# Layer norm deviations by one pow, token rows in one store, and a new order of the first rounds in a vision tower kernel

## The chip, the core and the metric

The kernel runs on one NeuronCore of a Trainium2 chip, as one program. The metric is device time in microseconds, the median of several executions. TensorE is called PE here, VectorE DVE, ScalarE ACT, GpSimd POOL and SyncE SP.

## What is computed

```python
h = tok(x, ...)                          # 16 images x 256 tokens x 512 features, an SSM kernel as token mixer
h = concat([cls_tok, h], axis=1)         # 16 x 257 x 512
h = h + attn(layernorm(h), ...)          # gates = ln(u) @ W_in + b; scan over tokens; @ W_out; plus u @ W_skip
h = h + ffn(layernorm(h), ...)           # 8 experts, 2 per token, and a shared expert

def layernorm(x, eps=1e-5):
    return (x - mean(x)) / sqrt(var(x) + eps)
```

The attention step normalises once more: its own layer norm acts on the already normalised row. With v the variance of a row, the first norm divides by sqrt(v + eps), and the second by sqrt(v/(v + eps) + eps).

## The kernel before, in words

Three parts run one after the other. **Setup** (lines 283 to 523) converts all weights of the attention step and of the shared expert into pairs of f16 halves (SP loads, ACT makes the high half, DVE the low half, line 480), builds tables for the token mixer, and ends in a barrier of all engines. SP's last work in it is to write the 7 blocks of empty rows of `x_slots` (lines 303 to 310): seven stores of zeros, a wait, seven stores of 128 single words each, a wait.

**Rounds** (from line 706): every engine runs `body(k)` for k = -1 to 17. Rounds 2 to 13 are a loop, the others are unrolled. `iterate` (line 629) does this. Chunk n of 256 rows (chunk 0: 128 rows with the class token) passes through several rounds:

- in round n-2 the token mixer makes it: DVE computes tables `tok_e` (line 1225) and products `tok_p` (line 1247, six steps f = 0 to 5), PE multiplies (`features`, line 942), ACT copies the result to `hst` (`tok_out`, line 1116), SP stores it to `h_tok` in HBM (line 795);
- in round n-1 SP loads it back as `hx` (line 760), DVE takes its statistics (`stats2`, line 1397), POOL works out the deviations (lines 850 to 859, ten instructions that wait for each other, three of them pow), DVE normalises (line 1445), ACT and DVE split it into f16 halves (`x2r`, lines 1161 and 1450), PE transposes and multiplies with `W_in`, and DVE scans (`scan`, line 1325);
- in round n PE multiplies with `W_skip` and `W_out` (`project`), DVE adds the residual `hc` with the factor `ir` (lines 1467 and 1468), takes statistics for each tile of 128 rows, POOL works out the deviation (lines 882 to 884), DVE normalises (`normed`), ACT and DVE split (`rows_hi`, `rows_lo`), PE transposes, and the router follows;
- in round n+1 PE and ACT run the shared expert, DVE chooses the experts (`choose`, `place`), and POOL scatters the rows to `x_slots` with indirect DMAs (line 872).

Each engine's order is written out by hand in `body`, and semaphores join them. ACT's order in a round is: silu(0) (activation of the shared expert's columns), the high half of yT, silu(1), the copy of `ir`, the residual copy `hx` to `hc` (line 1149, semaphore `c_prom`), the rest of the shared expert, `x2r`, and so on. SP may only overwrite `hx` with the next chunk when `c_prom` says that the copy is done, when the store of that chunk has landed (`c_hst`), and when `c_lo2` says that the old chunk is split. Behind this load on SP's queue stand the store of converted expert weights and the loads of the next ones.

**Experts** (from line 1085): 71 tiles of 128 rows, with transposing loads, matmuls, and an indirect DMA that adds to the result. The change does not touch them, nor the final copies to `out`.

## Time and profile before

| what | value |
| --- | --- |
| median of 3 runs | 1319.91 us (1319.89 to 1320.18) |
| the profiled execution | 1316.03 us |
| its span, which the rows count from | 1314.3 us |
| setup | 0 to 61.9 us |
| round -1, to the start of scan(0) | 61.9 to 91.4 us |
| round 0, from there to scan(1) | 91.4 to 131.0 us |
| round 1 | 131.0 to 174.2 us |
| rounds 2 to 13, the loop | about 44.1 us each |
| experts' first matmul | 859.8 us |

Times in rows are microseconds from the start of the span unless a column says ns. A line number is that of the kernel before. Where one row joins several instructions, x says how many. What stands in square brackets at the end of a row is how long the engine stood idle before it, and which instruction released it.

### The profile page before, as it was taken

The numbers are of one execution on the slowest core, as the hardware profiler recorded it, in microseconds if no ns is written. First come the engines' busy times: TensorE is split into PE (matmuls) and PEld (weight loads), VectorE is DVE, ScalarE is ACT, GpSimd is POOL, SyncE is SP. The second block draws the span as 40 slices with busy tenths as digits, with TensorE's granted clock in tenths as the row PEclk, the third lists the DMA queues.
The fourth block names the chain that finished last, engine by engine and source line by source line (L and its number), as shares of the span: only waits on it lengthen the run. The fifth ranks groups of instructions, "written<-read, shape, count | busy, mean of one in ns | idle before, by whom it ended". The sixth has DMA issues, their size and how long they took to land.

```text
span 1314.3 us, 28311 instructions
## 1 busy us (share of the span) xinstructions
PE 1096.3 (83%) x8330; PEld 720.8 (55%) x8331; DVE 847.0 (64%) x2171; ACT 356.6 (27%) x675; POOL 459.0 (35%) x519
## 2 busy tenths in 40 slices
PE   2045799998999899989999998769999999999970
PEld 2034467566655765676567755535555555555540
DVE  7855788888888888888888765524344444444440
ACT  4312243324332433244324432201111111111110
POOL 1012321432143224322432231115555555555550
PEclk8556899999999999999999999889999999999995
DMA  5510233333333323332333239659997788878868
GB/s 181 153 32 17 75 107 110 97 116 115 101 110 117 115 86 122 120 115 76 129 123 116 81 127 406 238 134 177 218 195 132 127 129 131 132 128 133 131 95 264
DMA packets 238515, 174.51 MB, mean 133 GB/s; under 512 B 186162, under 2 KB 204978, under 8 KB 236164
## 3 DMA queue, kind: packets, MB, share of 16 engines
q1 hardware_dynamic: 221924, 128.54, 37.7%
q0 software_dynamic: 15504, 36.46, 13.9%
q10 hardware_dynamic: 1040, 8.91, 1.7%
q8 instruction: 25, 0.41, 0.1%
q14 instruction: 22, 0.18, 0.1%
HBM read 61.59 MB, written 88.12 MB: 114 GB/s over the span
## 4 chain that ended last, share of the span: by engine, by line
PE 40%; DVE 26%; issue 10%; DMA 6%; ACT 4%; POOL 3%; SPq 2%; POOLq 1%; DVEq 1%; ACTq 0%
PE bank L1077 9%; PE bank L1067 9%; PE bank L1068 8%; PE bank L930 6%; PE bank L1011 4%; DMA mixed<-h_tok 3%; DVE wexp L1257 3%; DVE wexp L1273 2%; DVE h L1467 2%; DVE h L1468 2%; DVE stat L1470 2%; POOL sc L882 1%; DVE wexp L1237 1%; DMA sums<-x2w,rows_in 1%; PE bank L952 1%
## 5 line engine op out<-in xcount | busy, mean ns | idle before, releaser
L930 PE MATMUL bank<-wexp 128*128 128x256 f16 (+2 forms) x3252 | 419.7, 288 | 26.0 <-DVE gf L1280 13.7
L930 PEld LDWEIGHTS bank<-wexp 128*128 128x128 f16 x3252 | 309.0, 100 | 114.3 <-issue 20.5
L1067 PE MATMUL bank<-wexp,rows_in 128*128 x852 | 256.0, 313 | 10.8 <-issue 4.5
L1068 PE MATMUL bank<-wexp,rows_in 128*128 x852 | 255.4, 313 | 0.0
L908 POOL DMA_INDIRECT sums<-x2w,rows_in x71 | 113.8, 1602 | 119.8 <-DMA sums<-x2w,rows_in 76.0
L896 POOL TENSOR_TENSOR ex<-base,ld 128x8 f32<-128x8 f32 x71 | 120.5, 1697 | 80.4 <-DVE ld L1512 80.0
L1533 DVE SCALAR_TENSOR_TENSOR mixed<-bank,mixed 128x352 f32<-128x352 f32 x71 | 37.3, 525 | 163.0 <-ACT mixed L1214 126.5
L1011 PE MATMUL bank<-wexp 128*128 128x512 f16 x495 | 112.5, 380 | 17.0 <-DVE wexp L1273 15.5
L1067 PEld LDWEIGHTS bank<-wexp,rows_in 128*128 128x128 f16 x852 | 83.2, 98 | 69.2 <-issue 29.4
L850 POOL TENSOR_SCALAR sc<-mv 128x2 f32<-128x2 f32 x17 | 5.5, 321 | 317.6 <-DVE mv L1409 317.6
L1214 ACT ACTIVATE mixed<-bank 128x352 f32<-128x352 f32 x71 | 32.9, 463 | 304.7 <-PE bank L1068 285.3
L1077 PE MATMUL bank<-wexp,gates 128*128 (+1 forms) x477 | 111.7, 379 | 3.2 <-DMA gates<-mixed 1.7
L1068 PEld LDWEIGHTS bank<-wexp,rows_in 128*128 128x128 f16 x852 | 83.3, 98 | 44.0 <-issue 0.3
L872 POOL DMA_INDIRECT x_slots<-x3w,sl x66 | 81.1, 1229 | 70.9 <-DVE sl L1323 40.3
L1011 PEld LDWEIGHTS bank<-wexp 128*128 128x128 f16 x495 | 45.8, 98 | 73.6 <-issue 16.8
L1125 ACT ACTIVATE sgs<-bank 128x256 f32<-128x256 f32 (+1 forms) x102 | 38.1, 373 | 157.5 <-PE bank L930 157.5
L1257 DVE TENSOR_TENSOR wexp<-wexp 128x1024 f32 (+1 forms) x64 | 77.9, 1220 | 2.3 <-issue 1.9
L1077 PEld LDWEIGHTS bank<-wexp,gates 128*128 128x128 f16 (+1 forms) x477 | 46.6, 98 | 53.3 <-issue 4.5
L938 PE MATMUL bank<-ident,x2w 128*128 128x128 f16 x264 | 18.9, 228 | 65.6 <-DVE x2w L1450 54.8
L952 PE MATMUL bank<-wexp 64*128 64x64 f32 x1024 | 68.8, 290 | 4.4 <-DVE wexp L1262 4.4
L882 POOL TENSOR_SCALAR sc<-mv 128x1 f32<-128x1 f32 x33 | 22.9, 694 | 134.6 <-DVE mv L1472 134.6
L952 PEld LDWEIGHTS bank<-wexp 64*128 64x128 f32 x1024 | 66.5, 206 | 4.9 <-DVE wexp L1262 4.9
(250 smaller groups left out, 1469.2 us busy)
## 6 DMA issues: line engine op xcount, KB each, us to landing
w_halves<-rows_in SPq DMA_DIRECT2D x16, 704.0 KB
wexp<-w_halves ACTq DMA_DIRECT2D x1, 8704.0 KB
wexp<-w_halves SPq DMA_DIRECT2D x8, 1088.0 KB
h_tok<-tokens SPq DMA_DIRECT2D x128, 64.0 KB, 2.5
mixed<-h_tok SPq DMA_DIRECT2D x16, 512.0 KB, 4.2
sums<-r_o SPq DMA_DIRECT2D x16, 512.0 KB, 2.8
out<-sums SPq DMA_DIRECT2D x16, 512.0 KB, 11.0
x_slots<-zrow SPq DMA_DIRECT2D x8, 792.0 KB, 11.9
```

Source lines behind the costliest of these rows:

```text
L872: nc.gpsimd.indirect_dma_start(out=xs_d.bitcast(I32), out_offset=bass.IndirectOffsetOnAxis(ap=sl[:, i, c:c + 1], axis=0), in_=x3w[:, i, :] ...
L896: nc.gpsimd.tensor_tensor(ex[:, b % 2, 0, :], base[:], ld[:, b % 2, :], ALU.pow).then_inc(d_ex, 1)
L908: nc.gpsimd.indirect_dma_start(out=rs_d, out_offset=bass.IndirectOffsetOnAxis(ap=ext[b][:, E:E + 1].bitcast(I32), axis=0), in_=yo[b % 2][: ...
L930: last = MM(dst, stat_of(step, a), mov_of(step, b), start=(s_ == 0 and a + b == 0), stop=(s_ == len(steps) - 1 and a == 1))
L952: last = MM(BU[t][:, j * NA:(j + 1) * NA], pp[q, f, j].rearrange("p b c -> p (b c)"), ea[q, f, j, :], start=(f == 0), stop=(f == 1))
L1011: MM(BD[:], gT[:, m, a, t], wsd[:, m, b, :], start=(m == 0 and a + b == 0), stop=False)
L1067: MM(GB[:, 0:H], xT[b][:, a, c, :], wexp[:, u, o:o + H], start=s_, stop=e_)
L1068: last = MM(UB[:, 0:H], xT[b][:, a, c, :], wexp[:, u, o + H:o + 2 * H], start=s_, stop=e_)
L1077: last = MM(DB[:], gT2[b % 4][0:HK[c], a, c, :], wexp[0:HK[c], bass.ds(unit, 2), o:o + D // 2], start=(c == 0 and a + w == 0), stop=(c == ...
L1125: A(sgs[P - p1:P, m % 2, 0:w], BU[m % 2][0:p1, 0:w], ACT.Silu, scale=SXW).then_inc(c_sg, 1)
L1257: ch.do(TT((pp, pt)[f % 2][:, f // 2], cc, hh, ALU.mult))
L1533: STT(gx[:], UB[:, 0:H], SXW, sg[:], ALU.mult, ALU.mult).then_inc(d_gf, 1)
```

## The change

What it does, in eight edits:

- **One pow.** DVE computes `var2`, two columns for each of two tiles: v(1 + eps) + eps squared, and v + eps, with two `tensor_scalar` instructions behind the statistics. POOL takes one pow with exponent -0.5 over all four. The result's first half is the combined deviation of both norms. In place of ten POOL instructions there is one. The factor `SX` moves into the split: ACT's copy scales, and DVE's subtraction becomes `scalar_tensor_tensor`. The same for the second norm of a chunk: `var3` on DVE, one pow on POOL, for each tile.
- **ir on DVE.** The residual's factor is made by two DVE instructions ahead of `scan`, in place of pow, multiply (POOL) and copy (ACT).
- **One store of tokens.** `h_tok` is laid out so that each of the 128 partitions of `hst` writes one run of 4 KB: one DMA in place of eight. The load back then reads runs of 256 B in place of 2 KB, in two DMAs.
- **Residual copy first.** ACT copies `hx` to `hc` at the head of its round.
- **First features first.** In round -1 DVE does all six `tok_p` steps of chunk 1 directly behind the statistics of chunk 0 and ahead of its normalisation, PE does `features` at the head of the round, and ACT does `tok_out` at the head of the round. `tok_e(1)` moves from ahead of the round to ahead of the statistics.
- **Empty rows early.** Two stores (one of 1.8 MB, one of 64 B runs) ahead of the weight loads in place of fourteen behind them.
- DVE's and POOL's waits on buffers that no longer exist go.
- The counts of chained instructions per loop round follow (POOL 14 to 1, DVE 47 to 49).

The core of the diff:

```diff
+                sp.wait_ge(p_gp, 17)
+                none = xs_d[ZERO:ZERO + ZT * P, :].bitcast(I32).rearrange("(z p) w -> p z w", p=P)
+                sp.dma_start(none[:, :, 0:D], zrow[:].bitcast(I32)[:, 0:D]...broadcast_to([P, ZT, D])).then_inc(p_z, 16)
+                sp.dma_start(none[:, :, D:D + 16], zt[:]).then_inc(p_z, 16)
                 for i, (kind, src, n) in enumerate(jobs):
...
-                for z in range(ZT):
-                    sp.dma_start(none[:, z, :], zrow[:].bitcast(I32)).then_inc(p_z, 16)
-                sp.wait_ge(p_z, 16 * ZT)
-                for z in range(ZT):
-                    sp.dma_start(none[:, z, D + E:D + E + 1], zt[:, z:z + 1], allow_slow_non_contiguous=True).then_inc(p_z, 16)
-                sp.wait_ge(p_z, 32 * ZT)
+                sp.wait_ge(p_z, 32)
# SP: load and store of tokens
-                        sp.wait_ge(c_hst, n * NB * 16)
+                        sp.wait_ge(c_hst, n * 16)
-                        sp.dma_start(hx[:], src).then_inc(c_hx, 16)
+                        src = hs_d[bass.ds(n - 1, 1)].rearrange("q b i p a -> p (q i) b a")
+                        for i in range(2):
+                            sp.dma_start(hx[:, i, :].rearrange("p (b a) -> p b a", a=NA), src[:, i]).then_inc(c_hx, 16)
...
-                        for b in range(NB):
-                            sp.dma_start(dst[b], hst[b * B:(b + 1) * B].rearrange("c j t a -> c (j t) a")).then_inc(c_hst, 16)
+                        dst = hs_d[bass.ds(n - 1, 1)].rearrange("q b i (c t) a -> (q b i c) (t a)", t=TC)
+                        sp.dma_start(dst, hst[:].rearrange("p j t a -> p (j t a)")).then_inc(c_hst, 16)
# POOL
-                        link(TS(sc[:, 0, :], mv[:, 0, :, 1], EPS, None, ALU.add))
-                        link(TT(sc[:, 1, :], sc[:, 0, :], pwc[:, 0, :], ALU.pow))
...
-                        TS(sc[:, 3, :], sc[:, 3, :], SX, None, ALU.mult).then_inc(c_pw2, 1)
+                        TT(inv2[:], var2[:], power[:], ALU.pow).then_inc(c_pw2, 1)
...
-                            link(TS(sc[:, 5, i:i + 1], mv[:, 1, i, 1:2], EPS, None, ALU.add))
-                            link(TT(sc[:, 6, i:i + 1], sc[:, 5, i:i + 1], pwc[:, 0, 0:1], ALU.pow))
-                            TS(sc[:, 6, i:i + 1], sc[:, 6, i:i + 1], SX, None, ALU.mult).then_inc(c_pw3, 2 // nt)
+                            TT(inv3[:, i:i + 1], var3[:, i:i + 1], power[:, 0, 0:1], ALU.pow).then_inc(c_pw3, 2 // nt)
# PE
+                    if isinstance(k, int) and k == -1:
+                        features(k)
...
-                    if htok(k + 2):
+                    if htok(k + 2) and not (isinstance(k, int) and k == -1):
                         features(k)
# ACT
-                    A(x3r[:, i, 0, :], xf[:, i, :], ACT.Copy).then_inc(c_hi3, 2 // nt)
+                    A(x3r[:, i, 0, :], xf[:, i, :], ACT.Copy, scale=SX).then_inc(c_hi3, 2 // nt)
...
                 def body(k):
+                    if isinstance(k, int) and k == -1:
+                        tok_out(1, 0)
+                        tok_out(1, 1)
+                    if has(k):
+                        n, nt = k, tiles(k)
+                        act.wait_ge(c_hx, (n + 1) * 32)
+                        at_least(act, c_oev, n * 2)
+                        A(hc[:, 0:nt, :], hx[:, 0:nt, :], ACT.Copy).then_inc(c_prom, 1)
                     if has(k - 1):
                         silu(k - 1, 0)
...
-                        act.wait_ge(c_hx, (n + 1) * 16)
-                        act.wait_ge(c_pw2, n + 1)
-                        at_least(act, c_oev, n * 2)
-                        A(ir[:], sc[:, 4, :], ACT.Copy).then_inc(c_irc, 1)
-                        A(hc[:, 0:nt, :], hx[:, 0:nt, :], ACT.Copy).then_inc(c_prom, 1)
# DVE
-                        last.then_inc(c_st2, 1)
+                        last.then_inc(c_vr2, 1)
+                        v.wait_ge(c_vr2, n + 1)
+                        TS(var2[:, 0, :], mv[:, 0, :, 1], 1.0 + EPS, EPS * EPS, ALU.mult, ALU.add)
+                        TS(var2[:, 1, :], mv[:, 0, :, 1], EPS, None, ALU.add).then_inc(c_st2, 1)
...
+                        if m == 0 and isinstance(k, int) and k == -1:
+                            for f in range(5):
+                                tok_e(1, f)
                         if m == 0 and has(k + 1):
                             stats2(k + 1)
+                        if m == 0 and isinstance(k, int) and k == -1:
+                            for f in range(6):
+                                tok_p(1, f)
...
-                        TT(x2r[:, 0:nt, 1, :], xf[:, 0:nt, :], x2r[:, 0:nt, 0, :], ALU.subtract).then_inc(c_lo2, 1)
+                        STT(x2r[:, 0:nt, 1, :], xf[:, 0:nt, :], SX, x2r[:, 0:nt, 0, :], ALU.mult, ALU.subtract).then_inc(c_lo2, 1)
...
-                            nc.vector.bn_aggr(mv[:, 1, i, :], stat[:, 1, i, :]).then_inc(c_st3, 2 // nt)
+                            nc.vector.bn_aggr(mv[:, 1, i, :], stat[:, 1, i, :]).then_inc(c_vr3, 2 // nt)
+                            v.wait_ge(c_vr3, n * 2 + (i + 1) * 2 // nt)
+                            TS(var3[:, i:i + 1], mv[:, 1, i, 1:2], EPS, None, ALU.add).then_inc(c_st3, 2 // nt)
...
                     if has(k + 1):
+                        link(STT(irt[:], inv2[:, 0, :], SXW, inv2[:, 1, :], ALU.mult, ALU.mult))
+                        link(TT(ir[:], irt[:], var2[:, 0, :], ALU.mult))
                         scan(k + 1)
```

## Rows read from the trace of the kernel before

**Rows 1.** The page: granted PE clock by slice, and the chain's shares by engine.

```profile
PEclk8556899999999999999999999889999999999995
...
PE 40%; DVE 26%; issue 10%; DMA 6%; ACT 4%; POOL 3%; SPq 2%; POOLq 1%; DVEq 1%; ACTq 0%
```

**Rows 2.** Busy time in one loop round: length, PE, PEld, DVE, ACT, POOL, clock, DMA.

```profile
483.90:528.00 44.10, 40.44 (x358) 28.44 (x357) 36.78 (x84) 15.75 (x30) 13.68 (x21) 1.00 0.34 110
```

**Rows 3.** Setup, SP: the stores of single words (timeline), and one load (DMA issues).

```profile
57.23 3.18 SPq L309 DMA_DIRECT2D x_slots<-zt  x7
...
st<-in_L_attn_W_in SPq DMA_DIRECT2D x1, 768.0 KB, 10.2
```

**Rows 4.** Timeline at the end of setup: ACT's last work, DVE's last work, DVE's next.

```profile
54.82 3.92 ACT L367 ACTIVATE wexp<-pe 128x1024 f32<-128x1024 f32 x2
...
57.04 0.69 DVE L480 SCALAR_TENSOR_TENSOR wexp<-xj,wexp 64x512 f16<-64x512 f32 x1
61.95 0.07 DVE L1496 MEMSET carry<- 128x16 f32 x1 [4.22 <-PEq L189]
```

**Rows 5.** Timeline of round -1: normalisation of chunk 0, features of chunk 1, scan(0).

```profile
75.64 0.55 DVE L1445 TENSOR_SCALAR wexp<-mixed,mv,sc 128x512 f32<-128x512 f32 x1 [4.78 <-POOL sc L859]
...
80.37 7.09 PE L952 MATMUL bank<-wexp 64*128 64x64 f32 x64 [1.17 <-DVE wexp L1262]
...
91.41 0.23 DVE L1330 TENSOR_SCALAR gates<-gates 128x128 f32<-128x128 f32 x1 [2.52 <-ACT gates L1200]
```

**Rows 6.** Timeline of round 0: store and load of chunk 1, its statistics, normalisation, scan(1).

```profile
88.60 5.29 SPq L795 DMA_DIRECT2D h_tok<-tokens  x8
95.84 0.40 SPq L760 DMA_DIRECT2D mixed<-h_tok  x1
...
99.48 1.29 DVE L1402 BATCH_NORM_STATS2 stat<-mixed 128x6 f32<-128x512 f32 x2 [3.77 <-DMA mixed<-h_tok]
...
108.30 1.00 DVE L1445 TENSOR_SCALAR wexp<-mixed,mv,sc 128x512 f32<-128x512 f32 x2 [4.89 <-POOL sc L859]
...
131.03 0.29 DVE L1330 TENSOR_SCALAR gates<-gates 128x256 f32<-128x256 f32 x1 [5.62 <-ACT gates L1200]
```

**Rows 7.** Windows with a load alone, then a store alone; last columns DMA share, GB/s.

```profile
96.50:99.40 2.90, 2.90 (x9) 0.98 (x8) 0.00 (x0) 0.00 (x0) 0.00 (x0) 0.50 0.55 181
...
125.20:130.30 5.10, 5.10 (x48) 4.22 (x47) 0.21 (x1) 1.00 (x2) 0.00 (x0) 0.79 0.44 75
```

**Rows 8.** Groups by line and form: busy us, mean ns, idle before them.

```profile
L896 POOL TENSOR_TENSOR ex<-base,ld 128x8 f32<-128x8 f32 x71 | 120.5, 1697 | 80.4 <-DVE ld L1512 80.0
...
L1315 DVE TENSOR_TENSOR rt<-oh,rt 128x16 f32<-128x16 f32 x32 | 5.6, 175 | 1.1
```

**Rows 9.** Timeline of one loop round, by engine.

```profile
498.47 1.22 DVE L1257 TENSOR_TENSOR wexp<-wexp 128x1024 f32 x1
...
510.98 1.19 DVE L1262 TENSOR_TENSOR wexp<-wexp 128x1024 f32<-128x1024 f32 x1
513.55 0.55 DVE L1352 TENSOR_SCALAR wexp<-h,mv,sc 128x512 f32<-128x512 f32 x1 [1.38 <-issue]
...
520.91 0.55 DVE L1352 TENSOR_SCALAR wexp<-h,mv,sc 128x512 f32<-128x512 f32 x1 [1.30 <-POOL sc L884]
...
521.49 0.63 ACT L1114 ACTIVATE x3w<-wexp 128x512 f16<-128x512 f32 x1 [0.78 <-DVE wexp L1352]
...
497.97 0.71 POOL L855 TENSOR_TENSOR sc<-sc,pwc 128x2 f32<-128x2 f32 x1 [0.18 <-POOL sc L854]
...
502.05 0.22 POOL L859 TENSOR_SCALAR sc<-sc 128x2 f32<-128x2 f32 x1 [0.20 <-POOL sc L858]
...
511.29 0.98 POOL L882 TENSOR_SCALAR sc<-mv 128x1 f32<-128x1 f32 x1 [1.77 <-DVE mv L1472]
...
502.72 3.41 PE L1011 MATMUL bank<-wexp 128*128 128x512 f16 x15 [1.05 <-DVE wexp L1273]
```

**Rows 10.** Timeline of round 15: the statistics of the last chunk.

```profile
756.93 1.29 DVE L1402 BATCH_NORM_STATS2 stat<-mixed 128x6 f32<-128x512 f32 x2 [1.50 <-DMA mixed<-h_tok]
```

More of the change, by code:

```diff
@@ L45 @@
 UNROLL = 8
-PER_POOL, PER_DVE = 14, 47
+PER_POOL, PER_DVE = 1, 49
 def at_least(eng, sem, value):
@@ L550, in vit_tower @@
         mv = sb("mv", [P, 2, 2, 2], F32)
-        sc = sb("sc", [P, 8, 2], F32)
-        pwc = sb("pwc", [P, 2, 2], F32)
+        var2 = sb("var2", [P, 2, 2], F32)
+        inv2 = sb("inv2", [P, 2, 2], F32)
+        var3 = sb("var3", [P, 2], F32)
+        inv3 = sb("inv3", [P, 2], F32)
+        irt = sb("irt", [P, 2], F32)
+        power = sb("power", [P, 2, 2], F32)
         ir = sb("ir", [P, 2], F32)
@@ L1267, in tok_p, with tokens_p @@
                             ch.do(ins)
+                def tokens_p(k, f):
+                    if not isinstance(k, int) or k >= 0:
+                        tok_p(k + 2, f)
                 def glow(n, m):
```

59 lines of the change are left out of this document (22 added, 37 removed).

## The prediction

> **What bounds the kernel now.** I read the page first. Its chain of work is 40% PE and 26% DVE, with 10% "issue", 6% DMA and 3% POOL [rows 1]: no engine bounds the whole, so the change has to be priced stage by stage. The granted PE clock is at 0.5 in the second and third slices (33 to 98 us) and mostly full from the fifth [rows 1], so in the first rounds PE runs at its 1.2 GHz level. Then the timelines of each engine, stage by stage. *Setup*: ACT ends at 58.74 and DVE at 57.73, but the barrier opens only at 61.95, after SP's single-word stores that are issued until 60.41 [rows 3, 4]. *Rounds -1 and 0* are one serial chain: statistics, POOL's ten instructions, normalisation, features, store, load, statistics, POOL again [rows 5, 6]. *Loop rounds*: 44.1 us each, of which PE is busy 40.44 and DVE 36.78, and DVE's many short dependent steps leave it few real gaps [rows 2]. DVE and PE hand the path to each other: PE waits 1.05 us for a DVE result at 502.72, DVE waits 1.38 and 1.30 us for the second norm's deviation [rows 9]. *Experts*: untouched; they shift as a block.
>
> **Setup.** The empty rows leave the end. The barrier then waits for ACT (58.74) plus the 0.4 us that lie between the last store and DVE's start: DVE starts at 59.15, **-2.8 us**. The other side: 1.8 MB now stands ahead of the weight loads. At the 350 GB/s that loads reach this is about 5 us, with the 64 B runs about 6, so W_in lands at 22 and not 15.7 [rows 3]. What hides it: the beta matmuls and the last x transposes slip to about 26, ACT's second conversion to 28, and DVE asks for these halves only from 32.5 on; the loads of the second half of setup wait on DVE anyway. Cover left is some 6 us; past that it costs one for one. Floor: DVE's own end 57.73 gives -3.8; if cover fails, 0. SP waits for one more POOL memset and an iota (0.3 us), behind ten DMA issues: nothing.
>
> **Round -1.** DVE: statistics of chunk 0 come 1.15 us earlier in the order (one tok_p moves behind), so from 63.5; mean and variance are there at 64.65, two small instructions add 0.35, and six tok_p of 1.19 (the row at 510.98 is one) [rows 9] take 7.1: features can start at 72.15 instead of 80.37 and end 7.1 us later [rows 5], at 79.25. POOL's pow is finished under them. What is late next: ACT has tok_out ahead of x2r's high half, so that half waits until 80.35 although its input is ready at 72.7. Then 0.63 for it, 0.7 for the low half, 1.25 to the copy of the transposes, 1.0 for this copy, 3.3 for the W_in matmuls and 0.7 for tanh: scan(0) at 88.0 instead of 91.41 [rows 5], **-3.4 in all**.
>
> **Round 0.** The store (one issue) lands by about 85 and no longer matters. The load of chunk 1 now waits for the residual copy, which ACT reaches behind tanh: 88.0 to 88.6. Price of the load: before, 3.6 us from issue to statistics [rows 6], with 1.6 us of work per DMA engine (share 0.55 of 2.9 us, 256 runs of 2 KB, so 100 ns each) [rows 7]. A 256 B run costs 23 ns by the window with a store alone (share 0.44 x 16 x 5.1 us over 1530 runs) [rows 7], so 2048 runs take 3.0 us per engine: 2.0 fixed, 3.0, and 0.3 for the second issue give 5.3. Ends: 4.2, and 7.8 if a load of this grain goes at the pace of the eight stores (5.29 us plus landing) [rows 6]. I take 5.3, since the engine share is nearer to what limits one big DMA. Statistics at 93.95 (99.48 before). From there to the normalisation it was 8.82 us [rows 6], with ten POOL instructions. Now: 1.7 to the variance, 0.3 for var2, 2.33 for two tok_p, under which the pow of four columns (between 0.71 for two and 1.70 for eight [rows 8, 9], so 1.04) is hidden: 4.25. Normalisation at 98.2 instead of 108.30, -10.1; var3 in front of the last tok_p gives 0.1 back. scan(1) starts at 121.0 instead of 131.03 [rows 6]: **-10.0 in all**.
>
> **Round 1.** PE leads, partly at the lower clock. var2 (0.28) lies on the DVE stretch that feeds PE, and the two ir instructions (0.40) stand between the last split and scan(2): **+0.7**. The pow gains vanish behind PE and ACT.
>
> **A loop round.** DVE gains work: two var2 instructions after the wait (0.28), var3 twice (0.20 each), irt and ir (2 x 0.20), priced by dependent small ones of 0.175 plus 0.03 of hand-over [rows 8]. scalar_tensor_tensor costs what tensor_tensor did. What leaves: for the first tile the way from variance (511.06) to normalisation (513.55) [rows 9] was three POOL instructions. Now var3 ends at 511.26, tok_p runs to 512.37, and the pow ends up to 0.58 behind it. *Why not earlier*: the instruction at 511.29 takes 0.98 us where it needs 0.23, and it ends 0.10 after DVE's tok_p [rows 9]. POOL stands still while DVE reads two SBUF operands; a pow of 0.71 at most, held back like this, ends 0.71 - 0.23 + 0.10 behind. So 512.95, a gain of 0.6, and the same for the second tile (520.91). The Trainium skill, "SBUF — State Buffer", section "SBUF: two separate sides", says just this of a DVE instruction with two SBUF inputs, and more: the one that starts first holds the pair for the whole instruction, so a pow could stop DVE too.
>
> Now the path. irt and ir delay scan, hence gprod(0) and PE, by 0.40; var2 by another 0.28. PE waits for DVE's last glow (1.05) [rows 9] and then has no gap until features end, so features end about 0.7 later, and with them ACT's copies. Up to the first normalisation DVE is 0.68 late and gets 0.6 back: about even. The second one could be 0.6 early, but ACT, which splits it at 521.49, is busy with tok_out and the transposes until 521.35: only **-0.13** is left [rows 9]. Twelve loop rounds and round 14: -1.7. Bounds: -0.6 per round if PE's delay is absorbed, +0.4 if the small instructions cost half as much again and the tile gains are lost.
>
> **Hidden in the loop**: POOL's ten instructions, ready at 502.27 just before DVE wants them at 502.6 [rows 9]; the residual copy at ACT's head, which lies in 3.1 us of idle before silu(0); the load of hx, which can now go at 483 and is needed at 493.9, so 11 us of cover for 5.3; the expert weights' transfers behind it on SP, which only move forward by 5 us; the scatters, that start earlier.
>
> **End.** In round 15 the statistics wait 1.50 us for the load [rows 10]. The earlier copy takes that away; PE becomes the limit and lets 1.0 through. In round 16 nothing of DVE covers the second tile's deviation: 0.56. Together **-1.6**.
>
> **Sum** against the profiled execution: -10.0 + 0.7 - 1.7 - 1.6 = -12.6, so 1316.0 becomes 1303.4. The median of the runs lies 3.9 above the profiled one; the same step from it gives 1307.3.
>
> **Rivals.**
> 1. *PE absorbs the small DVE steps*, so that both tile gains count: -0.6 in 14 rounds instead of -0.13, 1301. For it: DVE's two stalls of 1.3 us are plain. Against: PE is busy 40.44 of 44.1 [rows 2]. Chance 0.16.
> 2. *The rounds give back most of it*: +0.4 per round (7 us), or the start gains 5 less because the load takes 7.8 and the clock rises later: 1312 to 1317. Chance 0.16.
> 3. *DVE is stopped by the pow.* A four-column pow (1.04) that starts first would hold back the DVE subtraction beside it in each of 14 rounds: +15, 1322, no change. In the trace POOL's pow at 497.97 ran until 498.68 while a two-operand DVE instruction started at 498.47 and took its usual 1.2 us [rows 9], which speaks against it. The Trainium skill's page on SBUF named above would have it so. Chance 0.05.
> 4. *The price of a run is fixed* (slower than before). If a run of 256 B costs the 100 ns of a 2 KB run [rows 7], a load takes 2048/16 x 0.1 + 2 = 14.8 us. Up to 11 us it is hidden in the loop; above, each round pays: 3.8 x 14 = 53, and the start 9.5: 1370. Against it stand the 23 ns. The Trainium skill, "DMA: Bandwidth & Descriptors", asks in "Specifications" for 512 B or more, without a price for this case. Chance 0.05.
> 5. *The edit does not do what it says*: features first but the chain to scan(0) unchanged. It is counted in 2.
>
> **How the numbers follow.** Forecast 0.58 (1303 to 1312), rivals 0.16, 0.16, 0.05, 0.05. The range 1297 to 1318 leaves out rivals 3 and 4 and a tail of the first. A measurement of this kernel tells about 0.2% (2.6 us) from no change: faster 0.87, same 0.07, slower 0.06.
>
> **What would show it.** In the new profile: DVE's first memset at 59.2; features from 72; scan(0) at 88, scan(1) at 121; the load of chunk 1 issued at about 88.6 and landed 5.3 later; loop rounds of 44.0; the second-norm wait of DVE 0.7 us instead of 1.38; pow of four columns about 1.04 when free. Wrong if the rounds are longer than 44.5 or shorter than 43.6, if the load takes over 8 us, or if PE's clock rises at another place in round 0 or 1.

## The result, and the profile after

The changed kernel takes **1297.36 us** (median of 4 runs, 1294.98 to 1299.14) against 1320.05 for the kernel before beside it (4 runs, 1319.89 to 1320.32). The ratio is 0.983, with a 95% interval from 0.981 to 0.986. The profiled execution took 1296.02 us with a span of 1294.3. Forecast were -12.6 us, measured are -22.7 by the medians and -20.0 between the two profiled executions. The forecast's direction held. The time lies in the range of 1297 to 1318, but only 0.4 us above its lower end, and outside the 1303 to 1312 that the forecast itself had named as the likely outcome. One execution in the experiments (of p_pow) was slow, with 5728 us, and is left out of that kernel's ratio and median.

The page of the changed kernel shows granted PE clock and chain shares, as [rows 1] does for before:

```profile
PEclk8557999999999999999999998989999999999995
...
PE 51%; DVE 23%; issue 8%; ACT 3%; DMA 3%; SPq 2%; DVEq 1%; POOLq 0%; POOL 0%; ACTq 0%
```

POOL's 3% of the chain are gone, and PE has grown from 40% to 51% of a shorter chain. A loop round, with the columns of [rows 2]:

```profile
466.63:510.37 43.74, 40.53 (x358) 28.39 (x356) 37.66 (x89) 15.64 (x29) 9.49 (x8) 1.00 0.31 111
```

PE has the same work in a shorter round (40.53 of 43.74 us), DVE has 0.9 us more, POOL 4.2 us less. The start, in rows that answer to [rows 4 to 6] (timeline, all engines, in order of time):

```profile
59.37 0.07 DVE L1506 MEMSET carry<- 128x16 f32 x1 [1.61 <-PEq L189]
...
65.35 1.84 POOL L851 TENSOR_TENSOR inv<-var,power 128x4 f32<-128x4 f32 x1 [4.84 <-DVE var L1410]
...
72.00 0.54 DVE L1451 TENSOR_SCALAR wexp<-mixed,mv,inv 128x512 f32<-128x512 f32 x1
...
81.02 0.69 DVE L1456 SCALAR_TENSOR_TENSOR x2w<-wexp,x2w 128x512 f16<-128x512 f32 x1 [8.48 <-ACT x2w L1153]
...
88.84 0.23 DVE L1327 TENSOR_SCALAR gates<-gates 128x128 f32<-128x128 f32 x1 [3.12 <-ACT gates L1192]
...
89.32 1.01 SPq L765 DMA_DIRECT2D mixed<-h_tok  x2
...
93.60 1.29 DVE L1399 BATCH_NORM_STATS2 stat<-mixed 128x6 f32<-128x512 f32 x2 [0.47 <-DMA mixed<-h_tok]
...
97.74 1.00 DVE L1451 TENSOR_SCALAR wexp<-mixed,mv,inv 128x512 f32<-128x512 f32 x2
```

The normalisation of chunk 0 starts at 72.00 without a wait for POOL (4.78 us before, [rows 5]), and that of chunk 1 at 97.74 instead of 108.30. DVE stood idle for 8.48 us ahead of L1456: the low half of the split needs ACT's high half, whose input is ready from 72.5 on, and ACT has tok_out ahead of it, which waits for PE's features until 79.39.

The loop round in the changed kernel, answering to [rows 9]: DVE's two second norms, ACT's split of the second tile, the two pows, and PE's wait.

```profile
495.86 0.55 DVE L1349 TENSOR_SCALAR wexp<-h,mv,inv 128x512 f32<-128x512 f32 x1 [0.53 <-issue]
...
502.57 0.55 DVE L1349 TENSOR_SCALAR wexp<-h,mv,inv 128x512 f32<-128x512 f32 x1 [0.44 <-POOL inv L873]
...
501.67 1.08 ACT L1109 ACTIVATE tokens<-bank 128x512 f32<-128x512 f32 x2 [1.50 <-PE bank L941]
502.63 1.03 ACT L1167 ACTIVATE wexp<-bank 128x1024 f16<-128x1024 f16 x1
503.54 0.64 ACT L1105 ACTIVATE x3w<-wexp 128x512 f16<-128x512 f32 x1
...
494.39 1.38 POOL L873 TENSOR_TENSOR inv<-var,power 128x1 f32<-128x1 f32 x1 [5.85 <-DVE var L1480]
501.53 1.01 POOL L873 TENSOR_TENSOR inv<-var,power 128x1 f32<-128x1 f32 x1 [5.76 <-DVE var L1480]
...
485.68 3.41 PE L1000 MATMUL bank<-wexp 128*128 128x512 f16 x15 [1.06 <-DVE wexp L1270]
```

The waits of 1.38 and 1.30 us have shrunk to 0.53 and 0.44. And ACT's split of the second tile, which stood 0.78 us for DVE, now follows directly behind the copy of the transposes: what ends last there has changed from DVE and POOL to PE and ACT.

**Where the 20 us went**, by stage. All numbers are differences between the starts of DVE's first instruction of scan(n) in a trace; "loop" is the mean from scan(3) to scan(14). The second column of each kernel is a further execution of the same kernel, profiled with the last experiments.

| stage, us | before | before again | after | after again | forecast of the difference |
| --- | --- | --- | --- | --- | --- |
| first DVE work of round -1 | 61.95 | 62.04 | 59.37 | 58.73 | -2.8 |
| from there to scan(0) | 29.46 | 30.15 | 29.47 | 29.46 | -0.6 |
| round 0 | 39.62 | 39.59 | 31.19 | 31.36 | -6.6 |
| round 1 | 43.16 | 41.94 | 40.33 | 40.32 | +0.7 |
| round 2 | 44.40 | 45.03 | 43.74 | 43.72 | -0.13 |
| loop, each | 44.20 | 44.16 | 43.75 | 43.73 | -0.13 |
| round 14 | 41.90 | 42.00 | 42.22 | 42.20 | -0.13 |
| round 15 | 41.05 | 40.91 | 39.00 | 39.03 | -1.0 |
| scan(16) to the end of the span | 526.6 | 526.6 | 527.7 | 526.6 | -0.56 |

The start was forecast well in sum (-10.0 at scan(1), measured -11.0 and -12.2). The excess is in round 1 (-2.8 or -1.6 instead of +0.7), in the loop (-0.45 or -0.43 instead of -0.13 per round) and in round 15 (-2.0 or -1.9 instead of -1.0).

### The profile page after: what moved, and what is told of

Read it like the earlier page. It is cut to its first block, busy times and chain, and to the rows that moved or that the text cites. A ratio compares the mean times of both kernels' runs of the same rounds, so it can differ in the third digit from the quotient of the medians.

```text
span 1294.3 us, 27562 instructions
## 1 busy us (share of the span) xinstructions
PE 1093.9 (85%) x8330; PEld 720.3 (56%) x8331; DVE 860.8 (67%) x2272; ACT 354.3 (27%) x658; POOL 387.5 (30%) x300
## 4 chain that ended last, share of the span: by engine, by line
PE 51%; DVE 23%; issue 8%; ACT 3%; DMA 3%; SPq 2%; DVEq 1%; POOLq 0%; POOL 0%; ACTq 0%
PE bank L1068 10%; PE bank L1058 9%; PE bank L1059 9%; PE bank L1000 8%; PE bank L919 7%; PE bank L941 5%; DVE wexp L1249 3%; DVE wexp L1270 3%; DVE rows_in L1497 2%; DVE stat L1399 2%; DVE wexp L1229 1%; DVE gf L1277 1%; SPq L754 1%; PE bank L927 1%; DMA x_slots<-x3w,sl 1%
## 5 line engine op out<-in xcount | busy, mean ns | idle before, releaser
L919 PE MATMUL bank<-wexp 128*128 128x256 f16 (+2 forms) x3252 | 416.2, 287 | 30.7 <-DVE gf L1277 15.9
L919 PEld LDWEIGHTS bank<-wexp 128*128 128x128 f16 x3252 | 307.8, 99 | 117.7 <-DVE gf L1277 24.1
L897 POOL DMA_INDIRECT sums<-x2w,rows_in x71 | 113.8, 1602 | 124.1 <-DMA sums<-x2w,rows_in 78.9
L1000 PE MATMUL bank<-wexp 128*128 128x512 f16 x495 | 112.5, 380 | 17.1 <-DVE wexp L1270 15.5
L864 POOL DMA_INDIRECT x_slots<-x3w,sl x66 | 93.6, 1418 | 88.7 <-DVE sl L1320 44.5
L851 POOL TENSOR_TENSOR inv<-var,power 128x4 f32<-128x4 f32 x17 | 19.1, 1121 | 328.2 <-DVE var L1410 328.2
L873 POOL TENSOR_TENSOR inv<-var,power 128x1 f32<-128x1 f32 x33 | 36.3, 1101 | 200.3 <-DVE var L1480 200.3
L1000 PEld LDWEIGHTS bank<-wexp 128*128 128x128 f16 x495 | 45.8, 98 | 73.7 <-issue 16.5
L1543 DVE TENSOR_TENSOR mixed<-mixed 128x352 f16<-128x352 f32 x71 | 37.3, 525 | 47.8 <-ACT mixed L1210 45.5
```

Source lines behind the costliest of these rows:

```text
L864: nc.gpsimd.indirect_dma_start(out=xs_d.bitcast(I32), out_offset=bass.IndirectOffsetOnAxis(ap=sl[:, i, c:c + 1], axis=0), in_=x3w[:, i, :] ...
L897: nc.gpsimd.indirect_dma_start(out=rs_d, out_offset=bass.IndirectOffsetOnAxis(ap=ext[b][:, E:E + 1].bitcast(I32), axis=0), in_=yo[b % 2][: ...
L919: last = MM(dst, stat_of(step, a), mov_of(step, b), start=(s_ == 0 and a + b == 0), stop=(s_ == len(steps) - 1 and a == 1))
L1000: MM(BD[:], gT[:, m, a, t], wsd[:, m, b, :], start=(m == 0 and a + b == 0), stop=False)
```

## The experiments

The last stage varies between executions of any of the kernels here: from the first to the 71st expert tile it takes 402.2 to 411.6 us, with no order by kernel (404.3 and 405.1 for before, 405.9 and 405.2 for after). So single times scatter by several us and the timed ratios are given with their intervals; causes are read from the stages ahead of it. The loop rounds repeat within 0.04 us between two executions of one kernel. The first rounds repeat less well: with the same instructions in them, round 0 took 39.62, 39.59, 39.86 and 38.65 us (before, before again, p_rows, w_keep), the stage to scan(0) 29.46 or 30.15, and round 1 43.16 or 41.94. This table has every kernel's stages, as above:

| kernel | first DVE work | to scan(0) | round 0 | round 1 | loop | round 15 | ratio to before (95%) |
| --- | --- | --- | --- | --- | --- | --- | --- |
| p_rows | 59.24 | 30.16 | 39.86 | 41.91 | 44.16 | 41.07 | 0.997 (0.994 to 1.000) |
| p_pow | 62.07 | 25.65 | 34.43 | 43.70 | 43.83 | 40.73 | 0.988 (0.982 to 0.994) |
| p_move | 62.43 | 30.16 | 36.94 | 41.66 | 44.09 | 39.72 | 0.997 (0.995 to 1.000) |
| p_feat | 62.15 | 28.85 | 39.34 | 41.89 | 44.18 | 41.03 | 0.998 (0.995 to 1.000) |
| e_split | 59.63 | 26.47 | 32.34 | 41.97 | 43.75 | 39.00 | 0.980 (0.978 to 0.982) |
| f_ir | 59.27 | 29.40 | 31.05 | 40.01 | 43.43 | 39.08 | 0.978 (0.976 to 0.981) |
| g_lock | 59.41 | 29.35 | 33.21 | 43.62 | 43.74 | 38.97 | 0.984 (0.982 to 0.986) |
| w_warm | 58.66 | 29.48 | 27.01 | 41.90 | 43.75 | 39.01 | 0.982 (0.979 to 0.984) |
| w_keep | 62.12 | 30.16 | 38.65 | 41.66 | 44.16 | 40.98 | 0.998 (0.996 to 1.000) |
| h_warm | 59.00 | 26.82 | 26.96 | 39.99 | 43.41 | 39.25 | 0.973 (0.970 to 0.976) |

### One part at a time

**Empty rows early, alone** (p_rows). Edit to the kernel before:

```diff
-                sp.wait_ge(p_z, 32 * ZT)
+                sp.wait_ge(p_z, 32)
```

with the eight stores of single words replaced by the two early ones of the change.

> The kernel before with the empty rows written early and nothing else. Theory: the end of setup moves alone, and everything behind it shifts as a block: first DVE memset behind the barrier at 59.4 instead of 61.95, scan(0) at 88.8 instead of 91.41, scan(1) at 128.4, round 1 and the loop rounds as before (43.2 and 44.2 us), so -2.6 us in all (about 1317.4). Rival 1: part of the setup's gain is lost behind later loads (W_in), then DVE starts later than 60. Rival 2: the shorter setup alone lets PE's clock rise earlier, then round 1 falls from 43.2 to about 40.3.

DVE starts at 59.24 and scan(0) at 89.40, both 2.8 us earlier than in before again, 2.7 and 2.0 earlier than in the first execution; the rounds behind are those of the second execution of before. The theory held for the setup; rival 2 fell, since round 1 (41.91) is that of "before again" and not 40.3.

**One pow per deviation, alone** (p_pow). The ten instructions on POOL become one, the additions and ir go to DVE:

```diff
-                            link(TS(sc[:, 5, i:i + 1], mv[:, 1, i, 1:2], EPS, None, ALU.add))
-                            link(TT(sc[:, 6, i:i + 1], sc[:, 5, i:i + 1], pwc[:, 0, 0:1], ALU.pow))
-                            TS(sc[:, 6, i:i + 1], sc[:, 6, i:i + 1], SX, None, ALU.mult).then_inc(c_pw3, 2 // nt)
+                            TT(inv3[:, i:i + 1], var3[:, i:i + 1], power[:, 0, 0:1], ALU.pow).then_inc(c_pw3, 2 // nt)
```

> The kernel before with the deviations alone changed (one pow each, the variance's additions and ir on DVE, the scale in the splits). Theory A (the loop's gain is the pow's): loop rounds of 43.7 to 43.8 instead of 44.2, the wait for the second norm's deviation 0.5 instead of 1.3, scan(0) 4 us and scan(1) 8 to 9 us earlier than before's 91.4 and 131.0, in all -14 to -18 us (1302 to 1306). Theory B (the loop's gain comes from the earlier load and the single store): loop rounds stay at 44.2, in all -9 us. The prediction's own sizing of the loop round (-0.13) would give rounds of 44.1. On the clock: if round 1 (43.2 before, 40.3 after) depends on how early PE's work of round 0 ends, it is shortened here too, since most of the 11 us at scan(1) are here; if it depends on the features' place, it stays at 43.

Theory A held: loop rounds of 43.83, scan(0) 3.7 and scan(1) 8.9 us earlier than in the first profile of before. The medians say -17.7 us (1301.20 of three executions against 1318.90), but with an interval of 0.982 to 0.994 and with the experts' scatter in them; the stages say less. At scan(16) p_pow is 12.1 us ahead of before, where the whole change is 21.1 ahead: the pow is the largest of the four parts, and somewhat over half. Its loop gain is the one of the change, give or take 0.1.

**Store, loads and residual copy, alone** (p_move).

```diff
-                        for b in range(NB):
-                            sp.dma_start(dst[b], hst[b * B:(b + 1) * B].rearrange("c j t a -> c (j t) a")).then_inc(c_hst, 16)
+                        sp.dma_start(dst, hst[:].rearrange("p j t a -> p (j t a)")).then_inc(c_hst, 16)
```

> The kernel before with the store in one transfer, loads in 256 B runs and the residual copy at the head of ACT's round, and nothing else. Theory: the load of chunk 1 is issued directly behind the residual copy, at about 92 instead of 95.8, and lands 4.3 us after its issue instead of 3.6, so scan(1) is 3.2 us earlier (127.8); loop rounds as before (44.2); round 15 loses its wait of 1.50 us for the load. In all -4.5 to -5 us (1315). Rival B (the loop's gain is from here): loop rounds 43.8, in all -10. Rival C (256 B runs are costly beside the expert weights' transfers): loop rounds longer than 44.4.

Round 0 is 2.65 us shorter than in before again and round 15 1.2 to 1.3. The loop comes to 44.09 with rounds that are all alike (44.07 to 44.14, where before has 44.10 to 44.31). Two rows show why, the load and the statistics behind it in a loop round of *before*:

```profile
489.26 0.40 SPq L760 DMA_DIRECT2D mixed<-h_tok  x1
...
493.47 1.29 DVE L1402 BATCH_NORM_STATS2 stat<-mixed 128x6 f32<-128x512 f32 x2
```

There are 4.21 us between them, where the load needed 3.64 behind its issue in [rows 6]: the cover was thin, and in some rounds (as from 400.85 to 405.21) it is 4.36, 0.15 more, and these rounds are longer. In p_move the load is issued 10 us ahead. So the move is worth 0.07 to 0.1 us per loop round; rival B, which had expected all of the loop's gain here, fell, and so did rival C.

**Features first, alone** (p_feat).

```diff
+                    if isinstance(k, int) and k == -1:
+                        features(k)
                     if has(k):
                         project(0)
```

> The kernel before with the features of chunk 1 first in the first round and nothing else. Theory: six tokens' instructions (7.1 us) now lie between statistics and normalisation and cover POOL's ten instructions, so the features start at about 75 instead of 80.4; scan(0), which waits for ACT's tok_out ahead of the split, gains 0.5 to 1; the eight stores are issued 5 us earlier and the load with them, so scan(1) is 3 to 5 us earlier; loop rounds 44.2 as before. In all -3 to -5 us. Rival: scan(0) is later than before, because the chain to it now has the features in front of it on DVE, PE and ACT, and the load waits for the residual copy anyway: then 0 or slower.

The first half held: features at 74.72, scan(0) 1.3 earlier behind DVE's start. The second fell: the load is issued at 94.51, because it waits for the residual copy and not for the stores, and round 0 gains only 0.3. In the whole change this part seems worse still. p_pow, without it, needs 25.65 us from DVE's start to scan(0), the changed kernel 29.47: with the pow short, nothing has to be covered any more, and the features stand in the way. This is argued from p_pow and e_split; the change without its features' move was not run.

At scan(16) the four parts alone stand 2.8 (p_rows), 12.1 (p_pow), 5.6 (p_move) and 2.0 us (p_feat) ahead of the first execution of before, 22.4 in sum against 21.1 for the whole. That they agree is in part chance: up to scan(0), behind DVE's start, p_pow gains 3.8 and p_feat 0.6 us, the whole nothing, and round 1 differs from trace to trace by the clock, as shown below.

### What the changed kernel's rounds wait for

**ACT's split ahead of tok_out** (e_split), in round -1 of the changed kernel:

```diff
-                    if isinstance(k, int) and k == -1:
-                        tok_out(1, 0)
-                        tok_out(1, 1)
...
                         A(x2r[:, 0:nt, 0, :], xf[:, 0:nt, :], ACT.Copy, scale=SX).then_inc(c_hi2, 1)
+                    if isinstance(k, int) and k == -1:
+                        tok_out(1, 0)
+                        tok_out(1, 1)
```

> The changed kernel, but in the first round ACT makes the high half of chunk 0's split (0.63 us) ahead of the two tok_out of chunk 1 instead of behind them. Theory: the changed kernel's way to scan(0) runs over ACT's order (tok_out 79.39, split 80.36), so scan(0) now follows the normalisation and not the features; but PE still has 7.1 us of features ahead of the transposes, so only the split's and DVE's subtraction leave the path: scan(0) 1.3 us earlier (87.5 instead of 88.84), the store 0.7 later, and with it nothing, since the load waits for the residual copy. scan(1) 0.6 to 1.3 earlier, loop rounds 43.75. Rival: PE's features were the limit alone, scan(0) within 0.3 of 88.84.

The direction was right and the size too small: from DVE's start to scan(0) 26.47 instead of 29.47, -3.0 us, and -1.9 at scan(1). PE's transposes follow the features without the 2.53 us of idle time that stood there (2.6 of the 3.0), since DVE's low half now lies under them, and the 36 W_in matmuls behind take 3.59 instead of 4.02 us (the other 0.4):

```profile
72.50 7.09 PE L941 MATMUL bank<-wexp 64*128 64x64 f32 x64 [45.63 <-DVE wexp L1254]
79.52 1.04 PE L927 MATMUL bank<-ident,x2w 128*128 128x128 f16 x8
```

**irt and ir on POOL** (f_ir), taken off DVE ahead of the scan:

```diff
-                        link(STT(irt[:], inv2[:, 0, :], SXW, inv2[:, 1, :], ALU.mult, ALU.mult))
-                        link(TT(ir[:], irt[:], var2[:, 0, :], ALU.mult))
                         scan(k + 1)
```

> The changed kernel with irt and ir computed on POOL at the end of its round (three small instructions) instead of on DVE ahead of the scan. Theory (the prediction's own step): 0.40 us of DVE ahead of the scan delays gprod(0) and PE by as much, and part of it reaches the round's length: loop rounds 43.5 to 43.6 instead of 43.75, 14 rounds, so -2 to -3 us. Rival 1: DVE's time there is covered, since PE's features and ACT's split come last either way: rounds 43.75 as before and 0. Rival 2: the whole 0.40 is on the path: rounds 43.35, -5.6 us.

Loop rounds of 43.43, -0.32 of the 0.40 taken away, and scan(16) is 4.75 us earlier than in the changed kernel. The prediction's reading that DVE's small steps ahead of the scan delay PE and are not covered is shown, nearly to their full size; round 14 returns to 41.91, so its +0.3 in the change (against 41.90) is these two instructions too.

**No two-operand DVE instruction beside the second norms' pow** (g_lock):

```diff
+                        if has(k) and i < tiles(k):
+                            normed(k, i)
                         if htok(k + 2) and i == 0:
                             tokens_p(k, 5)
                         if htok(k + 3) and i == 1:
                             tok_e(k + 3, 0)
-                        if has(k) and i < tiles(k):
-                            normed(k, i)
```

> The changed kernel with tok_p(5) and tok_e(0) placed behind the second norms' normalisation instead of between variance and normalisation. No DVE instruction with two SBUF operands then runs beside the pow of one column. Theory: this pow takes 0.58 to 0.62 instead of the 1.0 to 1.4 measured, DVE waits 0.7 us for it uncovered, the first tile's normalisation starts 0.9 earlier, and PE's features, which need tok_p(5), start 0.8 to 1.4 later; PE bounds the round, so the round gets 0.3 to 1.0 longer (44.1 to 44.7). Rival: the pow takes 1.0 or more here too, then it isn't the two-operand instruction that holds POOL up. Second rival: the round gets shorter than 43.75, then DVE's chain bounds it and not PE's.

One pow and the normalisation behind it, in g_lock:

```profile
506.19 0.54 POOL L873 TENSOR_TENSOR inv<-var,power 128x1 f32<-128x1 f32 x1 [6.09 <-DVE var L1480]
...
506.76 0.55 DVE L1349 TENSOR_SCALAR wexp<-h,mv,inv 128x512 f32<-128x512 f32 x1 [0.76 <-POOL inv L873]
```

Alone the pow takes 0.54 to 0.58 us, beside tok_p or tok_e 1.01 to 1.38 (rows of the changed kernel above): POOL is held up by DVE's two-operand instructions. The Trainium skill, "SBUF — State Buffer", section "SBUF: two separate sides", states that; the trace agrees for this direction. For the other one (a pow that is under way stops DVE) there is no sign. In round -1 of the changed kernel the pow of four columns ran from 65.35 to 67.19 beside the first of these three tok_p steps:

```profile
65.07 3.49 DVE L1249 TENSOR_TENSOR wexp<-wexp 128x1024 f32<-128x1024 f32 x3
```

The second of the three began at 66.20, with the pow under way, and took its usual 1.22 us.

The round's length did not move (43.74). That was in neither theory. The normalisation of the second tile is 0.96 us earlier in its round than in the changed kernel (34.98 against 35.94 behind the scan's start), and nothing follows from it, because ACT's split still stands behind tok_out and the copy of the transposes, and these behind PE's features, which start at the same place (31.08 and 31.10). PE runs from 485.68 to 501.56 in the changed kernel without a gap. So the loop's chain now is: DVE's last glow, 16 us of PE, ACT's three instructions, DVE's low half and the rest of its round. The pow is off it. (Rounds 0 and 1 of g_lock are 2.0 and 3.3 us longer than the changed kernel's; the next part shows the clock there.)

### The clock in rounds 0 and 1

Round 1 has one of three lengths in the traces without filled gaps in that round, and these go with two groups of 12 matmuls of 512 columns, those of project(0) and project(1), and with the stretches in which the granted clock was at the lower of its two levels (0.50 of full, 1.2 instead of 2.4 GHz). The second column gives these stretches in us behind scan(1), the last two rows are of the kernels with filled gaps in round 1:

| kernels | clock at the lower level | project(0), us | project(1), us | round 1, us |
| --- | --- | --- | --- | --- |
| after, after again, f_ir | 9.2 to 13.0 | 2.75 | 2.76 | 40.0 to 40.3 |
| before again, p_rows, p_move, p_feat | 24.1 to 27.9 | 2.75 | 4.1 to 4.3 | 41.7 to 41.9 |
| e_split, w_warm | 24.2 to 27.7 | 2.75 | 4.4 | 42.0, 41.9 |
| before, p_pow, g_lock | 10.0 to 17.1, and 27.1 to 30.7 | 4.6 to 4.7 | 4.1 to 4.2 | 43.2 to 43.7 |
| w_keep | 9.6 to 13.0 | 2.75 | 2.76 | 41.66 |
| h_warm | none | 2.75 | 2.77 | 39.99 |

These are rows of before, and of the changed kernel (PE, timeline), and the changed kernel's clock ahead of project(0) (windows, columns of [rows 2]):

```profile
144.14 4.57 PE L930 MATMUL bank<-wexp 128*128 128x512 f16 x12 [0.21 <-DVE sl L1321]
...
156.93 4.21 PE L930 MATMUL bank<-wexp 128*128 128x512 f16 x12 [2.38 <-DVE h L1468]
```

```profile
133.18 2.75 PE L919 MATMUL bank<-wexp 128*128 128x512 f16 x12 [0.20 <-DVE sl L1318]
...
144.40 2.76 PE L919 MATMUL bank<-wexp 128*128 128x512 f16 x12 [2.38 <-DVE h L1474]
```

```profile
129.60:132.90 3.30, 3.23 (x30) 2.77 (x27) 2.78 (x17) 0.47 (x2) 1.16 (x2) 0.50 0.00 0
```

So the changed kernel's clock falls in round 1 too, but ahead of project(0), where it costs nothing: project(0) starts 12.9 to 13.2 us behind scan(1) in every trace. What differs is where the fall lies. PE had the same gap of 2.38 us ahead of project(1) in before and in the changed kernel, and the clock was at its lower level behind it in one only, so this gap alone doesn't decide it. Why the fall lies early in some executions and late in others is not shown.

That gives a comparison of like with like for what the change does in round 1. With a late fall alone before's order takes 41.66 to 41.94 us (four traces) and the changed order 41.97 and 41.90 (e_split, w_warm): nothing is gained. With an early fall alone it is 41.66 (w_keep below, the only such trace of before's order) against 40.0 to 40.3. With both falls it is 43.16 (before) against 43.62 (g_lock). The lengths of round 0 go with the clock as well: it is at the lower level for 17 to 21 us of round 0 in the changed kernel's two executions and f_ir (31.05 to 31.36 us), for 24 in e_split and g_lock (32.34 and 33.21).

**PE's gaps filled in the changed kernel** (w_warm): matmuls nobody reads, 8, 10 and 12 at three places in rounds -1 and 0.

```diff
+                        for _ in range(count):
+                            MM(BD[:], wskip[:, 0, 0, 0:P], wskip[:, 0, 0, :], start=True, stop=True)
```

> The changed kernel with matmuls that compute nothing used (30 of 512 columns into an idle bank) in PE's gaps of the first two rounds: 8 behind the W_in matmuls of chunk 0, 10 behind project(0) of round 0, 12 ahead of its features. Theory (round 1's 2.8 us come from the granted clock): PE's clock then rises to its upper level by about 100 and not at 115; the features of round 0 take 3.6 to 3.9 us instead of 7.09 and the 36 matmuls behind them 2.8 to 4.2 instead of 4.95, so scan(1) comes 3.5 to 5.5 us earlier (115 to 116.5), round 1 stays near 40.3, in all -3.5 to -5.5 us. Rival: the clock doesn't follow PE's own work; then the added matmuls take 0.4 us each, features are delayed by up to 2 us and the kernel is 1 to 2 us slower.

The theory held in round 0. The features there (w_warm, PE) take 3.79 instead of 7.09 us:

```profile
105.90 3.79 PE L941 MATMUL bank<-wexp 64*128 64x64 f32 x64
109.62 0.62 PE L927 MATMUL bank<-ident,x3w 128*128 128x128 f16 x8
```

Round 0 is 4.2 us shorter (27.01) and scan(1) starts at 115.15. It was wrong for round 1: there the clock fell late, ahead of project(1) (4.35 us), and the round took 41.90. 1.6 of the 4.2 us went back, and the timed ratio is, within its interval, that of the change.

**One gap filled in the kernel before** (w_keep): 9 such matmuls ahead of project(1) of round 1.

```diff
+                    fill(k, 1, 9)
                     if has(k) and tiles(k) == 2:
                         project(1)
```

> The kernel before with 9 matmuls of 512 columns, whose result nobody reads, in PE's gap of 2.4 us ahead of project(1) in round 1 alone. In the kernels so far round 1 took 40.0 to 40.3, 41.7 to 42.0 or 43.2 to 43.7 us, and these differ by how many of its two groups of 12 matmuls of 512 columns took 4.2 to 4.6 us instead of 2.75. Theory: the gap ahead of project(1) lets the granted clock fall; with the gap filled project(1) takes 2.75 us and round 1 is 1.5 us shorter than the unchanged kernel's in the same call (40.2 or 41.7). Rival: the clock falls for another reason than PE's gap; project(1) still takes 4.2 and the round keeps its length or gets up to 1 us longer.

In this part of the round the clock stayed up: the filler is PE's first row here, and project(1) the second; the last two rows are windows, whose last column but two is the clock.

```profile
153.60 2.10 PE L971 MATMUL bank<-wexp 128*128 128x512 f16 x9
155.91 2.76 PE L930 MATMUL bank<-wexp 128*128 128x512 f16 x12 [0.20 <-DVE h L1475]
...
165.66 0.55 DVE L1359 TENSOR_SCALAR wexp<-h,mv,sc 128x512 f32<-128x512 f32 x1 [1.31 <-POOL sc L884]
...
140.60:143.90 3.30, 3.03 (x28) 2.50 (x25) 2.81 (x15) 0.49 (x3) 1.34 (x4) 0.50 0.40 140
153.60:158.70 5.10, 4.90 (x25) 2.07 (x23) 4.20 (x6) 0.00 (x0) 1.51 (x3) 1.00 0.28 108
```

That the filler did this is not shown by this run: the clock fell early here, ahead of any filler, and in the three unfilled traces with an early fall alone project(1) took 2.76 us too. More for the filler speaks h_warm below, where round 1 has no fall at all. But whatever kept the clock up, the round lost only 0.28 us (41.66 against 41.94), not the 1.4 that project(1) became shorter: the third row has DVE wait 1.31 us for POOL's deviation, and ACT's split waited 0.99 behind it, 1.37 us of PE idle in all. In before again, with project(1) at 4.18 us, DVE's wait for the same deviation is 1.30. In the kernel before, the clock's fall lay under the deviation's chain; in the changed kernel the same fall costs 1.6 us (e_split and w_warm against after).

**The further executions** (r_before, r_after), the two kernels unchanged.

> The kernel before once more, profiled. Theory: round 1's 43.2 us in the first profile hold one fall of the clock more (12 matmuls of project(0) at 4.57 us) than the kernel usually has, since three kernels with small edits elsewhere had 41.7 to 41.9; so 41.7 to 41.9 here. Rival: 43.2 again, then it belongs to the kernel. Experts' first tiles: first to 71st tile between 402 and 412 us, as in all kernels so far.

> The changed kernel once more, profiled. Theory: round 1 is 40.3 or, with a fall of the clock ahead of project(1), 41.9; loop rounds 43.75 and scan(1) at 120.0 (within 1.5 us) again; what varies between executions is round 1 and the experts' first tiles (402 to 412 us from the first to the 71st). Rival: loop rounds vary too, then -0.46 per round is no property of the change.

Both theories held, 41.94 for the first and 40.32 for the second. So 1.2 of the 2.8 us that round 1 seemed to gain belong to one execution of before. The other 1.6 need both the short deviation and a clock that doesn't fall late: e_split and w_warm, which have only the first, take 41.9 to 42.0, and w_keep, which has only the second, 41.66. Whether the change itself makes the early fall more likely is open. Round 2 was 45.0 to 45.2 in "before again", p_rows and w_keep, 44.3 to 44.4 in the other executions of before's order; the loop rounds repeat within 0.04.

### The terms together

h_warm is the changed kernel with ir on POOL, the split ahead of tok_out, and PE's gaps filled in rounds -1, 0 and 1 (the last 9 as in w_keep).

```diff
+                        if k == 1:
+                            bank = BU[1]
+                            pe.wait_ge(c_gm, k * 6)
+                        for _ in range(count):
+                            MM(bank[:], wskip[:, 0, 0, 0:P], wskip[:, 0, 0, :], start=True, stop=True)
```

> The changed kernel with irt and ir on POOL, ACT's split of chunk 0 ahead of tok_out, and matmuls whose result nobody reads in PE's gaps of rounds -1 to 1. If the terms add: scan(0) -1.9 (measured in the run with the split alone, less what its setup differed), round 0 -4.2 (measured in the run with the filled gaps), round 1 40.0, loop rounds 43.42 (-0.33 x 14 = -4.6): in all some 11 us below the changed kernel, 1286. Rival: round 1 keeps a low clock somewhere (41.6): 1288. Rival: the fillers delay real work, then round 0 is longer than 28.

The terms added, with round 1 free of any fall of the clock: scan(16) at 754.86, 11.7 us ahead of the changed kernel. **1282.46 us** (median of 6 runs), ratio to before 0.973 (0.970 to 0.976), below that of the changed kernel (0.981 to 0.986, timed at another time). Round 1 is 39.99 and the loop 43.41.

## Why the prediction was right, and where its terms were off

- **Setup** (-2.8; measured -2.6, -3.3 in the second execution). Right, with its cover: ACT's last work of setup ends at 59.05 and 58.41 (58.74 before), DVE's at 57.76 and 57.62 (57.73 before).
- **Features at 72.15** (72.23 measured) and **scan(0) at 88.0** (88.84): right up to PE, then 0.7 from the 36 W_in matmuls, which took 4.02 us where I had put 3.3.
- **What is late next** in round -1: named rightly (tok_out ahead of the split). e_split shows its price, 3.0 us. That the pow alone would bring scan(0) to 25.65 us behind DVE's start was not seen: I worked the features' move out only together with the pow, and so credited it with a gain that the pow had. The changed kernel's own stage to scan(0) (29.47) gained 0.0 on the first execution of before and 0.7 on the second, where 0.6 was forecast.
- **The load**: forecast 5.3 with bounds 4.2 and 7.8, measured 4.28. Windows from the load's first issue to the statistics, before and then in the changed kernel:

```profile
95.84:99.48 3.64, 3.64 (x10) 1.33 (x9) 0.00 (x1) 0.00 (x0) 0.00 (x0) 0.50 0.44 144
...
89.32:93.60 4.28, 1.46 (x4) 0.59 (x5) 3.16 (x10) 0.31 (x1) 0.00 (x0) 0.81 0.58 123
```

  Share times length gives 1.6 us of work per DMA engine before and 2.5 in the changed kernel for the same 512 KB, so 19 ns per run of 256 B (the prediction took 23) and 100 per run of 2 KB. The rest is 2.0 before and 1.8 here, where the prediction had 2.3: the 0.3 for the second issue is not seen. The Trainium skill, "DMA: Bandwidth & Descriptors", section "Specifications", asks for 512 B or more; the trace agrees, with half as much work again per engine, of which 0.64 us reach the statistics. The smaller price took 1.0 out of scan(1) and by luck made up for scan(0), which came 0.8 late.
- **Round 1** (+0.7; measured -1.6 against the second execution, -2.8 against the first). The step that failed is "The pow gains vanish behind PE and ACT". It holds where the clock falls ahead of project(1) (41.66 to 41.94 against 41.97 and 41.90), and there +0.7 was too much. It fails where it doesn't: then DVE and ACT in the kernel before still wait 1.31 and 0.99 us for the deviation (w_keep, 41.66), and the changed kernel, with the shorter deviation, takes 40.33 and 40.32. The fall lay early in both executions of the changed kernel and late in e_split and w_warm; why stays open. The prediction had named a changed place of the clock in round 0 or 1 as a sign of being wrong, and here it is.
- **The loop** (-0.13; measured -0.45 and -0.43). The mechanism was right, and each of its pieces can be found (medians of the loop rounds against before again, counted from DVE's first instruction behind the last rows_in step, which is irt in the changed kernel and the scan in the one before): PE's L1000 starts 0.64 later in its round (forecast 0.68), the first normalisation about even (-0.01), the second 0.65 earlier (forecast 0.6), f_ir gives 0.32 of 0.40 back. g_lock adds that the second normalisation no longer counts once ACT is behind PE. Off were the sizes. ACT's split of the second tile came 0.27 earlier and not 0.13, because in the rows an ACT instruction directly behind another starts 0.12 us ahead of the other's recorded end (503.54 against 502.63 + 1.03). Another 0.1 lies behind DVE's low half, where an idle time of 0.23 us has gone, and 0.07 to 0.1 came from the load, which I had counted as hidden on both sides, although a row of SP (489.26, above) would have shown only 4.2 us from its issue to its use.
- **Round 15** (-1.0; measured -2.05 and -1.9). p_move alone gives -1.2 to -1.3 and p_pow -0.2 to -0.3. The 1.50 us of [rows 10] went nearly whole: "PE becomes the limit and lets 1.0 through" was too careful. The two alone give 1.4 to 1.6 of the 1.9 to 2.05; the rest is not accounted for. The -0.56 of round 16 cannot be told from the scatter of that stretch (76.7 to 78.9 us from scan(16) to POOL's first pow of the experts, in all traces).
- **The rivals.** *PE absorbs the small DVE steps* gave nearly the measured time (1301) for a wrong reason: f_ir shows that PE does not absorb them. *The rounds give back* and *DVE is stopped by the pow* were not seen. *A fixed price per run* is excluded by 4.28 us and 19 ns per run.
- **In all**, the forecast of -12.6 was little more than half of what was measured (-20.0 and -22.7). Right was where the start gains and that the loop is shorter; the sizes of round 1, the loop and round 15 were all put too low, and of these the 1.6 us in round 1 hang on where the clock fell.

## What to carry to other kernels

A wait that is removed is worth what stands behind it, and a profile shows only the uppermost of two limits: the clock's fall ahead of project(1) cost 0.28 us under the deviation's chain (one trace against one) and 1.6 without it. Profile a kernel twice before a difference in its first rounds is put down to a change. Price two edits of one chain apart as well as together; here the features were moved ahead to cover POOL's ten instructions, and when these became one the move had nothing left to cover (p_pow reaches scan(0) in 25.65 us, the whole change in 29.47). Small dependent instructions ahead of the engine that bounds the round cost nearly their full time in every round (0.32 of 0.40), so put them on an idle engine, as f_ir does with POOL.

## What the runs showed of the hardware

- PE's clock can be held up by work of no use: 30 matmuls in its gaps brought 4.2 us in round 0 (w_warm, and h_warm again). With 9 more in round 1 h_warm had no fall of the clock there; w_keep, with the same 9, had one ahead of them.
- The same program sees its clock fall at different places: in before it was at its lower level from 10.0 to 16.8 and from 27.1 to 30.5 us behind scan(1) in one execution, and only from 24.4 to 27.8 in the next. Project(0) took 4.57 us in the one and 2.75 in the other.
- A pow of one column on POOL takes 0.54 to 0.58 us alone and up to 1.38 beside DVE instructions with two operands in SBUF, one of four columns 1.03 and 1.84. No DVE instruction was seen to be held up by a pow.
- Statistics on a load of 512 KB started 4.28 us after its first issue in runs of 256 B, and 3.64 us after its issue in runs of 2 KB. The work per DMA engine was 2.5 and 1.6 us, so 19 and 100 ns per run.
